# Queue orders in four places of a four-layer transformer kernel; the gate's exponential as a pow on GpSimd; gelu's table ahead of the norm; expert inputs halved off two banks

## The chip, the cores and the metric

One core of a Trainium2 chip runs the whole program as one launch. The metric is the device time in microseconds, as the median of several runs. TensorE (PE) multiplies matrices into PSUM banks of 128 x 512 f32; VectorE (DVE), ScalarE (ACT) and GpSimd (POOL) work element by element; SyncE (SP) issues the loads. Each engine works off its own queue in order and waits on semaphores.

## The reference, cut to what matters

The activations x are 2 x 256 tokens of 128 features, the context 2 x 512 x 128. Four layers follow one another, each a cross attention and a feed-forward part, all added to x:

```python
x = x + L0_xattn(layernorm(x), ctx, ctx, mask_ff1, ...)       # L0x: 16 heads of 64
x = x + L0_ffn(layernorm(x), tile_sigs, W, b)                 # L0f: one of 8 matrices per token
x = x + L1_xattn(layernorm(x), ctx, ctx, mask_bk0, ...)       # L1x: 16 heads of 8
x = x + L1_ffn(layernorm(x), ...)                             # L1f: self-attention, then 8 experts
x = x + L2_xattn(layernorm(x), ctx, ...)                      # L2x: 16 heads of 64
x = x + L2_ffn(layernorm(x), ...)                             # L2f: quantised product
x = x + L3_xattn(layernorm(x), ctx, ctx, ...)                 # L3x: one head of 128
x = x + L3_ffn(layernorm(x), ...)                             # L3f: small attention on 31 tokens
```

The parts that the change touches:

```python
# L0_ffn
scores = einsum('bsd,td->bst', x, sign(tile_sigs)); idx = argmax(scores, -1)
out = take_along_axis(einsum('bsd,tde->bste', x, W) + b, idx)
# L1_ffn
x = x + layernorm(attention(x, ...)) * ln1_g + ln1_b
probs = softmax(xt @ gate_w + gate_b)            # 8 experts
top_v, top_i = top_k(probs, 2); combine = sum(one_hot(top_i) * top_v)
for e in range(8):
    h = gelu(xt @ W1[e] + b1[e]) @ W2[e] + b2[e]
    out = out + combine[:, e:e + 1] * h
```

## The kernel before, in words

All work is laid out by hand: each engine has one program (`@block.tensor` and so on), and a stage is a function on each engine that runs in the order of the calls. There is no planner. `take` gives TensorE a PSUM bank once its last reader has freed it; `filled` and `emptied` are the two waits on a bank; `spare` issues products whose result nobody reads, in order to keep TensorE busy.

Tokens lie as 4 tiles of 128 rows (`X`, `XN`), or transposed as 128 x 512 (`XT`). The banks are S0 to S3, T0, T1, O and M. Products whose precision matters are made of f16 halves: a "high" is the value cast to f16 (ScalarE, `act_high`), a "low" is the rest (VectorE, `low`), and `PARTS` multiplies high by high, low by high and high by low, three passes into one bank. GpSimd's `split` makes both halves with two instructions: a product by one, and a subtraction.

The places that the change touches, in order of time:

- **Starts of L0x and L2x** (`pe_attention`, `project` L454, `pair_scores` L474, call at L575). TensorE makes the keys of the second pair of heads, K0(0,1), and then the scores of the first pair (j = 0 and 2). VectorE takes the maxima (L1668 in L2x) or looks for zeros (L1683 in L0x); in L2x it then halves the keys (L1703, L1708).
- **L0f and the way into L1x** (`pe_columns`, `pe_signatures`, `pe_l1x_kv`, `pe_l0f`, `pe_l1x`; VectorE's `l0f`, `l1x`). TensorE transposes bias columns, signs and four weights (bank T0), ScalarE copies the weights (L1459), TensorE projects the context to keys L1x.k0 and k1 (S0, S1). Then come the transposes of the normed rows (L867), the routing scores (L876), 8 routed products y0 to y7 (L889), VectorE's routed sum (L1901, 32 instructions). The keys are halved into `KN` by ScalarE (high) and VectorE (`l1x_low`); `pe_early_keys` repeats them for 4 heads at a time (RK, 8 pieces, L630), and ScalarE copies each out (L645). L1x's norm: VectorE's statistics, GpSimd's rstd (L2374, a pow by -0.5), VectorE's normed rows (L1605). Between statistics and normed rows VectorE has `small_loads` and the low of L2's value piece V0. TensorE then transposes (L385), fill value 2, query, fills 3 and 4, and the repeat of the query (RQ0, L654). GpSimd's queue: split of the routing weights, rstd of L0f, `selectors` (three memsets, six casts), rstd of L1x, then the splits of seven filled values, from a ring of four buffers `V32`.
- **Start of L1f** (`pe_l1f` L922): transposes, 6 spares, query, key and value projections, then `pe_packed`, which waits for the query, repeats it (RQ0), then repeats the key (RK0.0).
- **Into the experts** (`pe_l1f` L933 to L937, `act_moe` L1416, VectorE L1972 to L1984, GpSimd L2540 to L2547). The normed rows are transposed into bank M, ScalarE copies them to `XT[0]`, VectorE casts and subtracts (`halves`, L1629 and L1630) to get `X16`; TensorE computes the gate in f32 (L804), VectorE centres it (L1981) and finds the best expert (`best`, L1860 to L1864), ScalarE computes exp of the centred scores (L1418) and, per expert, gelu of four banks (L1426) and their highs (L1433); VectorE makes the lows (L1941) and splits W1 (L1947, L1949); GpSimd splits W2 (L2534, L2537) and adds the residual to X (L2545, L2547). VectorE finds the second expert, builds the factors (L1989 to L1996) and adds up (L2008, L2010).
- **Experts on TensorE** (`hidden` L946, `outputs` L958, `rounds`): hidden(i, k2 + 1), then outputs(i, k2). Five spares stand ahead of outputs(0, 0), four ahead of outputs(0, 1) and of the last outputs. `outputs` waits for all four hidden parts and goes token tile by token tile.

## Time and profile before

| | us |
|---|---|
| median of 3 runs | 552.6 (552.43 to 554.38) |
| the profiled execution | 552.83 |
| its span, first to last instruction | 551.1 |
| TensorE busy | 507.4 (92%) |
| VectorE busy | 432.0 (78%) |
| ScalarE busy | 341.0 (62%) |
| GpSimd busy | 271.3 (49%) |
| mean granted clock of TensorE | 0.994 |

Busy shares are means over stages with different limits. TensorE's figure includes the spare products. The stages in time: L0x until 148, L0f and the way into L1x until 180, L1x until 248, L1f's attention until 298, the experts until 355, L2x from 368 to 485, then L2f, L3x and L3f.

### The profile page before, as it was taken

What the parts mean: (1) busy time and instruction counts of PE and PEld (TensorE: products, weight loads), DVE (VectorE), ACT (ScalarE), POOL (GpSimd) and SP (SyncE); (2) the same over time, 40 slices, a digit from 0 to 9 for tenths busy, and PEclk for the clock granted to TensorE, in tenths of its full rate; (3) what the DMA queues carried; (4) which work ended last, traced back from release to release, by engine and by line L of the source; (5) the groups of instructions that cost most, each with busy time, mean ns of one, the idle gap of its engine ahead of it and who ended that gap; (6) DMA issues with size and microseconds to landing.
All of it is one profiled execution on the core that took longest, in us unless ns stands there. A gap on an engine that the chain in (4) does not pass through costs nothing.

```text
span 551.1 us, 13307 instructions
## 1 busy us (share of the span) xinstructions
PE 507.4 (92%) x4908; PEld 293.0 (53%) x4916; DVE 432.0 (78%) x1208; ACT 341.0 (62%) x682; POOL 271.3 (49%) x300
## 2 busy tenths in 40 slices
PE   8899999999897899999899799988999999999996
PEld 4345555567752233343334467735566656954574
DVE  7999999997584888827876899778777777587663
ACT  4688888888236366644662768538878888522212
POOL 7947777777622924410120443126888888500100
PEclk9989999999989999999999999999999999999999
DMA  9560000001120000000000222000000002000000
GB/s 236 133 175 8 1 2 3 1 2 41 51 103 1 1 1 2 2 1 0 2 1 21 77 77 58 2 1 1 2 1 3 1 2 78 3 0 1 2 0 20
DMA packets 24084, 15.43 MB, mean 28 GB/s; under 512 B 8083, under 2 KB 22230, under 8 KB 23894
## 3 DMA queue, kind: packets, MB, share of 16 engines
q1 hardware_dynamic: 24022, 14.60, 9.5%
q8 instruction: 39, 0.64, 0.5%
q14 instruction: 23, 0.19, 0.1%
HBM read 14.33 MB, written 0.26 MB: 26 GB/s over the span
## 4 chain that ended last, share of the span: by engine, by line
PE 51%; DVE 17%; issue 16%; POOL 9%; ACT 6%; DMA 1%; DVEq 0%; POOLq 0%; ACTq 0%
PE pspair L506 7%; PE psO L521 5%; PE psS L492 4%; PE psM L464 4%; PE pspair L967 4%; PE psO L720 3%; PE pspair L695 3%; DVE nmx L1788 2%; PE pspair L492 2%; ACT PP L1314 2%; POOL PP L2388 2%; PE pspair L954 2%; POOL PP L2385 2%; PE psS L669 1%; PE psS L954 1%
## 5 line engine op out<-in xcount | busy, mean ns | idle before, releaser
L506 PE MATMUL pspair<-ident,PP 128*128 128x128 f32 x512 | 82.1, 283 | 3.8 <-ACT PP L1314 3.7
L506 PEld LDWEIGHTS pspair<-ident,PP 128*128 128x128 f32 x512 | 54.2, 141 | 31.1 <-issue 21.7
L521 PE MATMUL psO<-V,PP 128*128 128x64 f16 x1536 | 65.7, 193 | 2.6 <-DVE Oall L1724 2.0
L521 PEld LDWEIGHTS psO<-V,PP 128*128 128x128 f16 x1536 | 59.8, 98 | 9.1 <-DVE PP L1690 2.9
L1690 DVE TENSOR_TENSOR PP<-pspair,PP 128x512 f16<-128x512 f32 x64 | 44.0, 688 | 25.7 <-ACT PP L1298 25.7
L1377 ACT ACTIVATE PP<-pspair 128x1024 f32<-128x1024 f32 x48 | 46.5, 1021 | 24.7 <-PE pspair L706 24.5
L2374 POOL TENSOR_TENSOR ln_rs<-ln_ve,minus_half 128x4 f32<-128x4 f32 x10 | 10.3, 1031 | 95.5 <-DVE ln_ve L1581 92.4
L1314 ACT ACTIVATE PP<-scores_m,nm 128x512 f32<-128x512 f32 x64 | 46.5, 727 | 5.5 <-DVE nm L1674 5.5
L2385 POOL TENSOR_TENSOR PP<-acc,one 128x512 f16<-128x512 f32 x32 | 33.3, 1040 | 31.7 <-ACT acc L1296 31.7
L2385 POOL TENSOR_TENSOR PP<-y_sb,one 128x512 f16<-128x512 f32 x32 | 33.3, 1040 | 16.9 <-ACT y_sb L1296 16.9
L2388 POOL TENSOR_TENSOR PP<-y_sb,PP 128x512 f16<-128x512 f32 x32 | 37.1, 1161 | 2.5
L2388 POOL TENSOR_TENSOR PP<-acc,PP 128x512 f16<-128x512 f32 x32 | 37.1, 1161 | 2.5
L1298 ACT CAST PP<-pspair 128x512 f16<-128x512 f32 x64 | 37.2, 581 | 0.6 <-PE pspair L506 0.6
L378 PE MATMUL pspair<-ident 128*128 128x512 f16 x136 | 34.3, 379 | 0.0
L464 PE MATMUL psM<-ctxTm,mask_i 128*128 128x512 f16 x99 | 27.5, 388 | 3.0 <-DVE Qst L1696 3.0
L1296 ACT COPY acc<-pspair 128x512 f32<-128x512 f32 x32 | 18.8, 587 | 13.2 <-PE pspair L506 13.2
L1296 ACT COPY y_sb<-pspair 128x512 f32<-128x512 f32 x32 | 18.8, 587 | 10.8 <-PE pspair L506 10.7
L720 PE MATMUL psO<-PP,Oall 128*9 128x256 f32 x384 | 25.2, 380 | 0.0
L1314 ACT ACTIVATE PP<-psS,nm 128x512 f32<-128x512 f32 x32 | 22.4, 699 | 3.5 <-DVE nm L1668 3.5
L1314 ACT ACTIVATE PP<-pspair,nm 128x512 f32<-128x512 f32 x32 | 22.3, 696 | 2.9 <-DVE nm L1668 2.9
L967 PEld LDWEIGHTS pspair<-scores_m,Oall 128*128 128x128 f16 x384 | 22.0, 98 | 2.2 <-issue 0.5
L1253 ACT COPY XT<-psM 128x512 f32<-128x512 f32 x7 | 4.1, 585 | 30.7 <-PE psM L385 30.7
(584 smaller groups left out, 1274.4 us busy)
## 6 DMA issues: line engine op xcount, KB each, us to landing
W<-in_L_ffn_W SPq DMA_DIRECT2D x16, 256.0 KB, 2.9
bigw<-in_L_xattn_w_q SPq DMA_DIRECT2D x2, 512.0 KB, 6.6
bigw<-in_L_xattn_w_kv SPq DMA_DIRECT2D x1, 1024.0 KB, 4.8
V<-in_ctx SPq DMA_DIRECT2D x1, 512.0 KB, 4.0
bigw<-in_L_xattn_w_v SPq DMA_DIRECT2D x1, 512.0 KB, 5.2
mask_b<-in_mask_BxS_ff SPq DMA_DIRECT2D x1, 512.0 KB, 7.1
bigw<-in_L_xattn_w_k SPq DMA_DIRECT2D x1, 512.0 KB, 6.1
bigw<-in_L_xattn_w_o SPq DMA_DIRECT2D x1, 512.0 KB, 3.9
```

The costliest lines, as they stand in the source:

```text
L464: mm = pe.matmul(bank["M"][:], (wq16 if what == "Q" else wk16)[:, wpart, cols_], X16[:, cpart, :] if what == "Q" else ctxTm16[:, cpart, keys],
L506: mm = pe.transpose(bank[f"T{j % 2}"][:, k * P:(k + 1) * P], Pb[j % 4][:, k * P:(k + 1) * P], ident[:])
L521: mm = pe.matmul(bank["O"][:, (j % UPH) * a.dv:(j % UPH + 1) * a.dv], (PTH, PTL)[ppart][j % 4][:, k * P:(k + 1) * P], (VH, VL)[vpart][:, b ...
L720: mm = pe.matmul(bank["O"][HR * j:HR * j + VR, b * S:(b + 1) * S], Vaug[:, b * kt + kc, HG * g + j, :], PX[(2 * r + j // 2) % 4][:, j % 2, ...
L967: mm = pe.matmul(bank[b][:, t * P:(t + 1) * P], HT16[k2][:, hpart, k, t * P:(t + 1) * P], W2h[k2][:, wpart, k * D:(k + 1) * D], start=(k = ...
L1296: nc.scalar.copy(P32[j // 2 % 2], ps[:]).then_inc(free[f"T{j % 2}"], 1)
L1298: nc.scalar.copy(PTH[j % 4][:, 0:a.keys], ps[:, 0:a.keys]).then_inc(sem(f"{n}.high"), 1)
L1314: nc.scalar.activation(Pb[j % 4][:, 0:a.keys], src[:, 0:a.keys], ACT.Exp, bias=nm[:, j % 4:j % 4 + 1], scale=-1.0 if a.mask else 1.0, accu ...
L1377: nc.scalar.activation(PX[k % 4], pairs[k % 2][:], ACT.Exp, scale=a.scale).then_inc(sem(f"{n}.exp"), 1)
L1690: dve.tensor_tensor(PTL[j % 4][:, 0:a.keys], ps[:, 0:a.keys], PTH[j % 4][:, 0:a.keys], ALU.subtract).then_inc(free[f"T{j % 2}"], 1)
L2385: pool.tensor_tensor(PTH[j % 4], P32[j // 2 % 2], one[:].broadcast_to([P, SK]), ALU.mult)\
L2388: pool.tensor_tensor(PTL[j % 4], P32[j // 2 % 2], PTH[j % 4], ALU.subtract)\
```

## The change

It reorders queues, moves work between engines and takes out spares. In the diff below "..." marks what is left out; left out are the removal of `l1x_low`, the allocation of `zero16`, `gate16` and `euler` and their two memsets on GpSimd, and the new bank names.

```diff
 def pe_attention
-            project("K0", 0, 1)
             for j in (0, 2):
                 pair_scores(0, j)
+            project("K0", 0, 1)
 def pe_early_keys
-                emptied(pe, f"L1x.k{c}")
+                pe.wait_ge(sem("L0.vsplit"), 5 + c)
 def pe_packed   (repeat of the key first, then of the query; ScalarE's copies likewise)
+            if halves:
+                emptied(pe, f"{n}.k")
+                repeat_k(pe, 0, 0, take(pe, f"{n}.RK0.0", "S3"), full["S3"])
+            emptied(pe, f"{n}.q")
+            ps = take(pe, f"{n}.RQ0", "S2")
+            repeat_q(0, ps, full["S2"])
 def pe_l1x_keys   (was pe_columns, pe_signatures, pe_l1x_kv)
             ...                                    # the four transposes of weights
             mm.then_inc(full["T0"], 1)
+            pe_columns(pe)
+            pe_signatures(pe)                       # bank T1, was S3
             emptied(pe, "L1x.wT")
             for g in range(2):
                 pe_one(pe, f"L1x.k{g}", f"S{g}", sqT[:, 1, :], ctxT[:, g * 512:(g + 1) * 512])
 def pe_l0f
-                    pe_early_keys(pe, range(0, 2))
+                    pe_early_keys(pe, range(0, 1))
...
             pe_onehot_rows(pe, "L0f", route_b)
+            pe_early_keys(pe, range(1, 3))
             pe_l1x_mask(pe)                         # bank S0, was T0
-            pe_early_keys(pe, range(2, 8))
+            pe_early_keys(pe, range(3, 8))
 def pe_l1x
-            pe_wide_values(pe, "L2", range(0, 2), "T0 T1")
+            pe_wide_values(pe, "L2", range(0, 1), "S1 S2")
...
             pe_ln(pe, "L1x", XN[0])
-            pe_fill_value(pe, 2, "S3")
+            pe_wide_values(pe, "L2", range(1, 2), "S1 S2")
             emptied(pe, "L1x.xt")
             pe_one(pe, "L1x.q", "M", sqT[:, 0, :], XT[0][:])
-            pe_fill_value(pe, 3, "S1")
+            pe_fill_value(pe, 2, "S3")
+            pe_fill_value(pe, 3, "S0")
             pe_fill_value(pe, 4, "T0")
 def pe_l1f
-            spare(pe, "T1", 6)
+            spare(pe, "T1", 4)
...                                                 # key, then query (was query, key)
             spare(pe, "S0", 16)
-            pe_ln(pe, "L1g", XN[0])
-            spare(pe, "S0", 3)
-            emptied(pe, "L1g.xt")
-            pe.wait_ge(sem("ld.moe"), 2 * 16)
-            pe_tiles(pe, "L1f.gate", "M", lambda t: XT[0][:, t * P:(t + 1) * P], lambda t: gate_w[:], E)
+            for h, b in enumerate(("M", "S3")):
+                ps = take(pe, f"L1g.xt{h}", b)
+                for t in range(2):
+                    pe.wait_ge(sem("L1g.xn"), 2 * h + t + 1)
+                    mm = pe.transpose(ps[:, t * P:(t + 1) * P], XN[0][:, 2 * h + t, :], ident[:])
+                mm.then_inc(full[b], 1)
+            spare(pe, "S0", 2)
+            for h in range(2):
+                emptied(pe, f"L1g.xt{h}")
+            pe.wait_ge(sem("gate"), 1)
+            ps = take(pe, "L1f.gate", "M")
+            for t in range(NT):
+                for m, (xpart, wpart) in enumerate(PARTS):
+                    mm = pe.matmul(ps[:, t * E:(t + 1) * E], X16[:, xpart, t * P:(t + 1) * P], gate16[:, wpart, :],
+                                   start=(m == 0), stop=(m == 2))
+            mm.then_inc(full["M"], 1)
+            def last_outputs(i):
+                b, base = at["moe.y1"]
+                pe.wait_ge(free[b], base + i)
+                pe.matmul(bank[b], zero16[:], ident16[:].unsqueeze(1).broadcast_to([P, 4, P]), start=True, stop=False)
+                pe.wait_ge(sem("moe.w2"), 2 * i + 2)
+                for k in range(NF):
+                    emptied(pe, f"moe.h{k}", 2 * i + 1)
+                    for t in range(NT):
+                        for m, (hpart, wpart) in enumerate(PARTS):
+                            mm = pe.matmul(bank[b][:, t * P:(t + 1) * P], HT16[1][:, hpart, k, t * P:(t + 1) * P],
+                                           W2h[1][:, wpart, k * D:(k + 1) * D],
+                                           start=False, stop=(k == NF - 1 and t == NT - 1 and m == 2))
+                mm.then_inc(full[b], 1)
...                                                 # used for the last expert; the spares of 5, 4 and 4 are gone
 ScalarE
-            act_high(act, f"L1x.k{g}", KN[:, g * 512:(g + 1) * 512])
+            act_copy(act, f"L1x.k{g}", V32[g])
-            nc.scalar.activation(pr8[:], sc8[:], ACT.Exp).then_inc(sem("moe.exp"), 1)
...                                                 # mask copy at n == 3, V0 and V1 behind L1x.xt, then the query
             act_out(act, L1F, 1)
-            act_copy(act, "L1g.xt", XT[0][:])
+            nc.scalar.activation(warm[:], one[:], ACT.Gelu)
+            for h in range(2):
+                act_high(act, f"L1g.xt{h}", X16[:, 0, h * 256:(h + 1) * 256], n=256)
 VectorE
-                ln("L1x", X, XN[0], [small_loads] + lows("L2", range(0, 1)))
-                wide_low("L2", 1)
+                ln("L1x", X, XN[0], [small_loads])
+                for step in lows("L2", range(0, 2)):
+                    step()
...
-                packed(L1X, [l3_angles])
+                packed(L1X, [l3_angles, gate_halves])   # gate_halves: gate_w to gate16, two instructions
...
-                emptied(dve, "L1g.xt")
-                halves(X16[:, 0, :], X16[:, 1, :], XT[0][:]).then_inc(sem("moe.x"), 1)
+                for h in range(2):
+                    low(f"L1g.xt{h}", X16[:, 1, h * 256:(h + 1) * 256], X16[:, 0, h * 256:(h + 1) * 256], n=256)
 GpSimd
+            selectors()
             rstd("L0f")
-            selectors()
+            pool.wait_ge(sem("L0f.factors"), 1)
+            for g, c in enumerate(halves):
+                emptied(pool, f"L1x.k{g}")
+                split(KN[:, c], KN[:, CTX + g * 512:CTX + (g + 1) * 512], V32[g], "L0.vsplit", g + 5)
             rstd("L1x")
...
-            pool.wait_ge(sem("moe.x"), 1)
+            for h in range(2):
+                emptied(pool, f"L1g.xt{h}")
             for k2 in range(2):
                 split_W2(0, k2, True)
+            pool.wait_ge(sem("moe.centred"), 1)
+            pool.tensor_tensor(pr8[:], euler[:].unsqueeze(2).broadcast_to([P, NT, E]), sc8[:], ALU.pow)\
+                .then_inc(sem("moe.exp"), 1)
```

## Rows read from the trace of the kernel before

**Rows 1.** The page, part 4: shares of the chain that ended last, by engine.

```profile
PE 51%; DVE 17%; issue 16%; POOL 9%; ACT 6%; DMA 1%; DVEq 0%; POOLq 0%; ACTq 0%
```

**Rows 2.** Timeline of VectorE, start of the first attention: start, us, engine, line, instruction, [idle before <-releaser].

```profile
25.20 1.29 DVE L1683 TENSOR_SCALAR Zt<-psS 128x512 bf16<-128x512 f32 x2 [0.22 <-PE psS L492]
```

**Rows 3.** Windows: length, busy us of PE, PEld, DVE, ACT, POOL, granted clock, DMA share, GB/s.

```profile
28.50:31.90 3.40, 3.40 (x14) 0.96 (x11) 2.27 (x8) 2.48 (x6) 0.00 (x0) 0.51 0.27 64
...
148.00:151.40 3.40, 1.92 (x11) 1.21 (x11) 3.17 (x18) 0.58 (x1) 0.55 (x1) 1.00 0.58 178
151.40:154.80 3.40, 3.40 (x10) 1.75 (x9) 1.02 (x4) 0.98 (x2) 3.33 (x10) 0.50 1.01 376
...
323.60:351.20 27.60, 27.60 (x309) 20.11 (x308) 26.12 (x52) 22.00 (x40) 10.85 (x10) 1.00 0.17 49
```

**Rows 4.** Timeline of TensorE from the end of the first attention on.

```profile
148.24 0.25 PE L827 MATMUL psO<-ident,vec 39*128 39x39 f32 x1
...
150.75 3.16 PE L809 MATMUL psS<-ctxT,sqT 128*128 128x512 f32 x4 [0.68 <-ACT sqT L1253]
...
173.85 1.01 PE L385 MATMUL psM<-ident,XN 128*128 128x128 f32 x4 [0.82 <-DVE XN L1605]
...
178.27 0.59 PE L654 MATMUL pspair<-qT,Oall 128*128 128x512 f16 x2
```

**Rows 5.** Timeline of VectorE, the same stages.

```profile
150.68 0.87 DVE L1872 TENSOR_SCALAR XN<-X,ln_mv 128x128 f32<-128x128 f32 x4
...
157.73 2.16 DVE L1901 SCALAR_TENSOR_TENSOR X<-psS,pr,X 128x128 f32<-128x128 f32 x8
...
172.75 0.69 DVE L1624 TENSOR_TENSOR V<-pspair,V 128x512 f16<-128x512 f32 x1 [3.96 <-ACT V L1260]
```

**Rows 6.** Timeline of GpSimd, the same stages.

```profile
151.82 0.96 POOL L2432 MEMSET Oall<- 128x1024 f32 x1
...
168.61 1.05 POOL L2374 TENSOR_TENSOR ln_rs<-ln_ve,minus_half 128x4 f32<-128x4 f32 x1 [13.81 <-DVE ln_ve L1581]
```

**Rows 7.** Timeline of ScalarE, the same stages.

```profile
170.09 1.26 ACT L645 ACTIVATE scores_m<-pspair,key_one 128x512 f16<-128x512 f32 x2 [0.20 <-PE pspair L630]
```

**Rows 8.** Timeline of TensorE, start of the self-attention (L1f).

```profile
253.46 1.02 PE L809 MATMUL psM<-XT,sq 128*128 128x512 f32 x2
...
258.57 0.40 PE L669 MATMUL psS<-Oall,Qst 24*128 24x256 f16 x4
```

**Rows 9.** Timeline of ScalarE, start of the mixture of experts.

```profile
306.00 1.28 ACT L1426 ACT_TABLE_LOAD   x1
```

**Rows 10.** Timeline of VectorE, the same stage.

```profile
303.86 0.69 DVE L1630 TENSOR_TENSOR XT<-XT 128x512 f16<-128x512 f32 x1
...
305.98 0.98 DVE L1861 TENSOR_TENSOR eq<-sc,rank 128x32 f32<-128x32 f32 x1
...
309.22 0.69 DVE L1941 TENSOR_TENSOR Oall<-psS,Oall 128x512 f16<-128x512 f32 x1
...
321.85 1.13 DVE L2008 TENSOR_SCALAR acc<-pspair,oh 128x128 f32<-128x128 f32 x4
```

**Rows 11.** Timeline of GpSimd, the same stage.

```profile
305.75 1.16 POOL L2537 TENSOR_TENSOR scores_m<-W,scores_m 128x512 f16<-128x512 f32 x1
```

**Rows 12.** Timeline of TensorE, the experts.

```profile
313.28 1.24 PE L378 MATMUL psM<-ident 128*128 128x512 f16 x5
...
351.26 1.03 PE L378 MATMUL psM<-ident 128*128 128x512 f16 x4
```

**Rows 13.** Groups of GpSimd instructions by form: count, busy us, mean ns.

```profile
L2374 POOL TENSOR_TENSOR ln_rs<-ln_ve,minus_half 128x4 f32<-128x4 f32 x10 | 10.3, 1031 | 95.5 <-DVE ln_ve L1581 92.4 <-DVE ln_ve L1578 3.2
...
L2566 POOL TENSOR_TENSOR ss<-ss,s_half 64x1 f32<-64x1 f32 x1 | 0.5, 541 | 21.6 <-DVE ss L2313 21.6
```

**Rows 14.** Timeline of TensorE, start of the last attention (L2x).

```profile
368.54 1.13 PE L468 MATMUL psM<-ctxT,bigw 128*128 128x512 f32 x2 [0.20 <-DVE Qst L1621]
```

**Rows 15.** Timeline of VectorE, the same stage.

```profile
370.46 1.29 DVE L1668 TENSOR_REDUCE nm<-psS 128x1 f32<-128x512 f32 x2 [1.97 <-PE psS L492]
```

More of the change, by code:

```diff
@@ L244, in build @@
         gate_w = sb("gate_w", [P, E])
+        gate16 = sb("gate16", [P, 2, E], F16)
+        euler = sb("euler", [P, 1])
         b2w = sb("b2w", [E, D])
@@ L732, in pe_packed @@
             halves = 0 if a.mask else B * a.keys // 512
-            emptied(pe, f"{n}.q")
             pe.wait_ge(sem("sel"), 5)
-            ps = take(pe, f"{n}.RQ0", "S2")
-            repeat_q(0, ps, full["S2"])
             if halves:
@@ L830, in pe_signatures, with pe_l1x_keys @@
             pe.wait_ge(sem("L0f.sign"), 1)
-            ps = take(pe, "L0f.sigT", "S3")
-            pe.transpose(ps[:, 0:E], signs[:, 1, :], ident[0:E, 0:E]).then_inc(full["S3"], 1)
-        def pe_l1x_kv(pe):
+            ps = take(pe, "L0f.sigT", "T1")
+            pe.transpose(ps[:, 0:E], signs[:, 1, :], ident[0:E, 0:E]).then_inc(full["T1"], 1)
+        def pe_l1x_keys(pe):
             pe.wait_ge(sem("ld.L1x"), 4 * 16)
@@ L853, in pe_l1x_mask @@
         def pe_l1x_mask(pe):
-            ps = take(pe, "L1x.mask", "T0")
+            ps = take(pe, "L1x.mask", "S0")
             pe.wait_ge(sem("mask"), 1)
@@ L859, in pe_l1x_mask @@
                                       mask_n[:, q, k * P:(k + 1) * P], identb[:])
-            mm.then_inc(full["T0"], 1)
+            mm.then_inc(full["S0"], 1)
         def pe_l0f(pe):
@@ L973, in rounds @@
                 for k2 in range(2):
-                    if not (last and k2 == 1):
-                        hidden(i, k2 + 1)
-                    else:
-                        spare(pe, "M", 4)
+                    if last and k2 == 1:
+                        last_outputs(i)
+                        continue
+                    hidden(i, k2 + 1)
                     outputs(i, k2)
-            pe.wait_ge(sem("moe.x"), 1)
             hidden(0, 0)
             hidden(0, 1)
-            spare(pe, "M", 5)
             outputs(0, 0)
             hidden(0, 2)
-            spare(pe, "M", 4)
             outputs(0, 1)
@@ L1377, in exps @@
                 nc.scalar.activation(PX[k % 4], pairs[k % 2][:], ACT.Exp, scale=a.scale).then_inc(sem(f"{n}.exp"), 1)
+            for c in range(halves):
+                repeated_k(0, c)
             repeated_q(0)
@@ L1381, in act_packed @@
                 act_fill_value(act, 5)
-            for c in range(halves):
-                repeated_k(0, c)
             for r in range(-a.lead, a.rounds + 2):
@@ L1473, in _ @@
                 act_repeated_k(act, Kaug, "L1x", n // 2, n % 2)
-            act_wide_values(act, "L2", range(0, 2))
             act.wait_ge(sem("ld.short"), 16 * len(SHORT))
@@ L1482, in _ @@
             act_copy(act, "L1x.xt", XT[0][:])
+            act_wide_values(act, "L2", range(0, 2))
+            act_high(act, "L1x.q", q16[:, 0:TOK], scale=float(DN) ** -0.5)
             act_fill_value(act, 2)
-            act_high(act, "L1x.q", q16[:, 0:TOK], scale=float(DN) ** -0.5)
             act_fill_value(act, 3)
@@ L1864, in best @@
                 return dve.tensor_tensor(dst[:], eq8[:], rank[:].unsqueeze(2).broadcast_to([P, NT, E]), ALU.is_equal)
-            def l1x_low(g):
-                low(f"L1x.k{g}", KN[:, CTX + g * 512:CTX + (g + 1) * 512], KN[:, g * 512:(g + 1) * 512])
             def l0f():
@@ L1956, in l1f @@
                 emptied(dve, "vec")
+                low("L1f.k", KN[:, CTX:CTX + TOK], KN[:, 0:TOK], bias=colp["L1_ffn_bk"])
                 low("L1f.q", q16[:, TOK:2 * TOK], q16[:, 0:TOK], bias=colp["L1_ffn_bq"])
-                low("L1f.k", KN[:, CTX:CTX + TOK], KN[:, 0:TOK], bias=colp["L1_ffn_bk"])
                 ps = filled(dve, "L1f.v")
```

21 lines of the change are left out of this document (11 added, 10 removed).

## Prediction

> **What bounds it now.** I read the page's chain of waits first. TensorE holds 51% of it, VectorE 17% and "issue" 16% [rows 1]; loads hold almost nothing. So the middle of each attention is TensorE's and the change hardly touches it; what it can win lies at the stage borders, where every engine waits on a chain of small steps. I then read the timeline of each engine around the six places that the diff touches, and the windows for the clock. The profiled execution took 552.83 us (span 551.1, 1.73 around it); the median of the three runs, 552.6, is 0.2 below it, so I sum against 552.83 and take 0.2 off. "Same" below means within 0.5% (2.8 us), about what a measurement of this kernel tells from no change.
>
> **1. Scores ahead of the key projection (L0x).** Before the first scores TensorE runs K0(0,1). VectorE starts on the scores at 25.20 after 0.22 idle [rows 2]; until then it drained values. The swap can give back only that 0.22; VectorE's queue is the next limit. The key's copy on ScalarE stands behind the first exp and isn't late. Term: -0.2. Bounds: 0 to -1.6, because at 28.50 to 31.90 the granted clock is 0.51 (the 1.2 GHz level) after a stretch in which TensorE mostly waited [rows 3]. The moved projection fills part of that wait. Were the clock to stay up, the half of the 3.4 us stretch that is lost would shrink until VectorE (busy 2.27 of 3.40 there) binds, about 1.35. I leave it out of the sum.
>
> **2. L0f and the start of L1x.** Four edits with one answer.
> Before: columns at 148.24, then the signatures' transpose waits for bank S3, the weights' transposes (0.66), ScalarE's copy, the two key projections at 150.75 for 3.16, so to 153.91 [rows 4]. The normed rows were begun at 150.68 and done at 151.55 [rows 5], so their transposes stood 2.2 us behind the keys. The keys are long since the clock was 0.50 in 151.40 to 154.80, after 1.92 busy of 3.40 [rows 3]; at full clock a pair of such passes takes about 0.86 (an estimate: two 512-column f32 passes take 1.02 with their overlapping end [rows 8]), so 1.7 for both.
> After: weights' transposes at 148.24 (no S3 to wait for), the two small ones beside ScalarE's copy, keys about 149.75. TensorE's wait shrinks from about 1.4 to 0.6, so I take it that the clock holds: keys done 151.5, normed transposes 151.95, scores, argmax, and the routed sum begins near 154.9 instead of 157.73 [rows 5]: -2.8. VectorE's two key rests leave its queue; they lay in waits.
> What pays: selectors() (0.96 memset first, 2.9 in all, from 151.82 [rows 6]) now runs from about 146.5, beside VectorE's mask preparation and the X additions. The rows show that VectorE's instructions with SBUF operands wait for a GpSimd instruction (item 5). Bounds 0 to +0.9 (memset alone); I take +0.4.
> The key halves go to GpSimd, behind L0f.factors: four instructions, 1.04 and 1.16 each by the same split elsewhere (the second is 1.16 [rows 11]; two instructions 1.12 apart), 4.5 us from 154.7 to 159.2. Cover: VectorE's routed sum reads PSUM, and L0f's rstd is ahead of them, L1x's far behind. First user is RK0.0 at about 158.7, which needs the first half (157.0): no wait. rstd for L1x follows in the queue and would start near 165.7.
> Then the larger half: rstd was ready at 168.61 + 1.05 = 169.66 [rows 6], but the normed rows stood in VectorE's queue behind the rest of V0, which ran only at 172.75 after 3.96 idle [rows 5]; TensorE transposed at 173.85 [rows 4]. Moved behind, that 3.7 goes. What is late next is ScalarE's key copies: the last pair ran 170.09 to 171.35 [rows 7], at 0.65 each; by the new order (mask third, banks S0) they end near 168.3, then three tiny activations, and the transposed copy at 168.95 (174.9 before). V1 stands ahead of the query on TensorE (0.86), fills 2 to 4 behind it (2.6). RQ0 comes at about 173.2 against 178.27 [rows 4]: -5.1, with the +0.4: **-4.7**. GpSimd starts splitting the fills 4 us sooner, so it stays ahead of its ring of four. Bounds: -2.8 (clock still low, selectors fully in the way) to -5.6.
>
> **3. L1f.** Spares 6 to 4 (0.43), key before query, its repeat first. From 253.46 (query) to the first narrow products at 258.57 [rows 8] is a chain of two projections, high, rest, repeat, copy. It starts 0.4 sooner; the last member is now the query, of the same form. **-0.4**, bounds 0 to -0.5.
>
> **4. Gelu's table.** Loaded at 306.00 for 1.28 [rows 9] between exp and the first gelu; now it runs in ScalarE's idle time behind the output copy, and exp is gone from ScalarE. First gelu near 304.8 instead of 307.30.
>
> **5. Halves of two banks, gate, pow.** X16 was ready at 303.86 + 0.69 = 304.55 [rows 10]; cast, copy and rest on two half tiles, the first under the second transposes, end about 303.6. Gate is 12 f16 products (about 0.45). Then VectorE binds: argmax instructions wait for GpSimd. The one at 305.98 took 0.98 [rows 10] and ended 0.05 after GpSimd's of 305.75 + 1.16 = 306.91 [rows 11]; uncontended such ones take 0.19. GpSimd's splits start 1.0 earlier and so end earlier; the first low, 309.22 [rows 10], comes at 308.4: only -0.8 of the 2.5 that gelu gained. The second hidden layer follows, and with the five spares at 313.28 (1.08 before the next product [rows 12]) gone, outputs(0,0) is 2.8 earlier. But the loop is VectorE's too (from 323.60 to 351.20 TensorE is busy for all 27.60, VectorE for 26.12 [rows 3]), and it enters it with the first sum, 321.85 [rows 10], which needs the factors. What sets those is GpSimd's new queue: split W2 twice (to 308.3), **pow**, X additions 2.6, W2 of the next expert 2.3.
> Pow on 32 elements isn't in the trace. 128x4 took 1.031, 64x1 0.541 [rows 13]: 0.163 per further element, so 0.54 + 31 x 0.163 = 5.6; below, 1.0 (all overhead), above 32 x 0.541 = 17.3. At 5.6 it ends at 313.9. The exponentials aren't needed before 319, but the two additions and the W2 split then fall on VectorE's W1(1,1) split and second argmax, which they hold up some 3 us where 1.6 were lost before. The first sum comes at 321.4: **-0.5**. At 1.0 the additions lie earlier: -2.0. If pow also holds VectorE's SBUF operands off for all its 5.6, W1(1,0) waits: +1.7.
> A rule of the Trainium skill bears here (SBUF — State Buffer, "SBUF: two separate sides" and "Who interferes with whom"): a GpSimd instruction that reads SBUF and a VectorE one with two SBUF inputs or in a two-port mode exclude each other for the whole instruction. The trace agrees for the argmax (0.98, not 0.19); by the rule alone pow would hold the port all along, which is rival A.
>
> **6. Last expert by k.** Zero product, then each hidden part as it comes. The four spares at 351.26 and the wait to 352.37 (1.1 [rows 12]) go, the zero product costs 0.2: **-0.9**, bounds -0.7 to -0.9. VectorE was waiting for that bank.
>
> **7. L2x.** Scores are 1.1 earlier (the projection of 368.54, 1.13 [rows 14]), the maxima too; but the key's copy, third on VectorE, now waits for the projection behind two pairs of scores, near 371.05 instead of 370.46 + 1.2 = 371.66 [rows 15]. **-0.6**, bounds 0 to -1.1.
>
> Two extra memsets at the start lie in a GpSimd wait. No load moves except with the stages.
>
> Sum: 0.2 + 4.7 + 0.4 + 0.5 + 0.9 + 0.6 = 7.3; 552.83 - 7.3 = 545.5, as a median 545.3. Ends of all terms: 11.7 and 1.8 saved (540.9 and 550.8).
>
> **Rivals.**
> A. Pow holds VectorE's SBUF port for its 5.6 us. For: the argmax rows. Against: the 128x4 pows run beside VectorE products of SBUF operands (L1587) that keep their length. Item 5 is +1.7 instead of -0.5: 547.5.
> B. L0f's gain is eaten: selectors delay X by 0.9, the clock stays at its low level, so item 2 is -2.8: 547.2. For: the clock fell there once. Against: less waiting ahead of it.
> C. Slower: pow costs its upper price, 17.3, and holds the port. W1(1,0), due at 310.9, ends at 326.7, where hidden(0,2) stood at 317.04 (313.28, 1.08 of spares, 2.68 of outputs): +9.7, and the lows, split and argmax queued behind it meet the additions (+2): +11.7 for item 5, less 6.8: 557.5. It beats the gain from a pow of about 12.5 us. Against: two points of pow lie far below.
> D. Both clock dips vanish and pow is short: 552.6 - 10.5 = 542.1.
> E. The gelu load isn't kept (copies between warm-up and gelu bring another table): item 4 back. VectorE binds there anyway, so about 0.5: 545.8, inside the forecast.
>
> **Chances.** Forecast (with E) 0.60, A 0.14, B 0.12, D 0.10, C 0.04. Its own range is 543.5 to 547; with A, B and most of D 541.8 to 549. Faster 0.89 (all but C and the worst joint cases of A and B), same 0.08, slower 0.03.
>
> **What would show it.** The routed sum 2.4 us earlier after the attention; clock 1.00 there; V0's rest behind the normed rows; no idle before XN beyond rstd; the pow's own row (near 5.6), VectorE's casts beside it either 0.42 or stretched; the table load before 300; no spares between the experts and 0.9 less before the last sum. Wrong would be: gaps before RK0.0 for the key halves, or a first sum later than before relative to the stage's start.

## The result, and the profile after

The changed kernel takes 546.88 us in the median of 7 runs (545.62 to 549.77). The kernel before, run beside it, takes 551.73 (551.40 to 554.38). The ratio is 0.991, with a 95% interval of 0.9884 to 0.9935: 4.9 us faster. I had forecast 545.3, in a range of 541.8 to 549. The profiled execution took 547.37 (span 545.7), 5.5 less than that of before, where the sum said 7.3. The ratios here and below leave out the few executions that took over 1.5% longer than the fastest of their kernel; the medians include them. All the differences below are between these two traces, each counted from its first instruction.

How far ahead of the kernel before the changed one is, at seven places:

| place | before | after | ahead |
|---|---|---|---|
| zeros of the third pair of heads, L0x | 32.12 | 31.00 | 1.12 |
| bias added to X, end of L0x | 147.55 | 147.55 | 0.00 |
| routed sum, L0f | 157.73 | 154.88 | 2.85 |
| repeated query RQ0, L1x | 178.27 | 172.93 | 5.34 |
| narrow products, L1f | 258.57 | 254.74 | 3.83 |
| first and last sum of the experts | 321.85, 355.25 | 317.88, 350.31 | 3.97, 4.94 |
| key copy of L2x | 371.66 | 366.22 | 5.44 |

VectorE after the last unit of L0x (start, us, engine, line, instruction, [idle before <-releaser]):

```profile
145.61 1.13 DVE L1680 TENSOR_SCALAR mask_n<-acc 128x512 bf16<-128x512 f32 x1
146.67 0.84 DVE L1680 TENSOR_SCALAR mask_n<-y_sb 128x512 bf16<-128x512 f32 x1
147.55 0.69 DVE L2382 TENSOR_TENSOR X<-X,rows 128x512 f32<-128x512 f32 x1
...
154.88 2.16 DVE L1923 SCALAR_TENSOR_TENSOR X<-psS,pr,X 128x128 f32<-128x128 f32 x8
...
166.85 1.12 DVE L1632 TENSOR_SCALAR XN<-X,ln_mv,ln_rs 128x128 f32<-128x128 f32 x4 [0.91 <-POOL ln_rs L2401]
...
364.50 1.29 DVE L1695 TENSOR_REDUCE nm<-psS 128x1 f32<-128x512 f32 x2 [0.94 <-PE psS L495]
366.22 0.69 DVE L1730 CAST Amat<-psM 128x512 f16<-128x512 f32 x1 [0.43 <-PE psM L471]
```

GpSimd beside it, and in the experts:

```profile
145.41 1.06 POOL L2459 MEMSET Oall<- 128x1024 f32 x1
...
154.70 1.05 POOL L2504 TENSOR_TENSOR kT<-ctxTm,one 128x512 f16<-128x512 f32 x1 [2.82 <-DVE oh L1891]
...
304.47 5.42 POOL L2578 TENSOR_TENSOR pr<-euler,sc 128x32 f32<-128x32 f32 x1
309.86 1.26 POOL L2582 TENSOR_TENSOR X<-X,XN 128x512 f32<-128x512 f32 x1
```

The third zeros and the mask instructions of the kernel before, for comparison:

```profile
32.12 1.29 DVE L1683 TENSOR_SCALAR Zt<-psS 128x512 bf16<-128x512 f32 x2 [1.35 <-PE psS L492]
...
146.75 0.43 DVE L1653 TENSOR_SCALAR mask_n<-acc 128x512 bf16<-128x512 f32 x1
147.09 0.42 DVE L1653 TENSOR_SCALAR mask_n<-y_sb 128x512 bf16<-128x512 f32 x1
```

The first memset now lies on VectorE's two mask instructions, which took 0.43 and 0.42 in the kernel before. They take 1.13 and 0.84, and the 1.12 that L0x had won is gone at 147.55. In L0f and L1x the picture is the forecast one. The normed rows stand behind rstd alone (0.91 idle, where 3.96 stood ahead of V0's rest [rows 5]), and the key halves on GpSimd keep nobody waiting.

TensorE, and the windows (length; busy us of PE, PEld, DVE, ACT, POOL; granted clock; DMA share; GB/s):

```profile
148.71 1.95 PE L812 MATMUL psS<-ctxT,sqT 128*128 128x512 f32 x4 [0.76 <-DVE X L2385]
...
172.93 0.59 PE L657 MATMUL pspair<-qT,Oall 128*128 128x512 f16 x2
...
249.74 1.10 PE L812 MATMUL psS<-XT,sq 128*128 128x512 f32 x2 [0.69 <-DVE V L1651]
250.67 1.02 PE L812 MATMUL psM<-XT,sq 128*128 128x512 f32 x2
...
305.43 2.54 PE L972 MATMUL psS<-XT,scores_m 128*128 128x512 f16 x6 [2.40 <-DVE Oall L1968]
```

```profile
25.20:28.50 3.30, 2.00 (x10) 0.56 (x9) 3.30 (x10) 1.04 (x3) 3.22 (x3) 1.00 0.59 135
28.50:31.90 3.40, 3.38 (x23) 1.98 (x24) 3.40 (x11) 3.19 (x9) 0.07 (x1) 1.00 0.28 68
...
179.40:182.80 3.40, 1.95 (x6) 0.53 (x6) 3.30 (x8) 0.58 (x1) 3.24 (x4) 1.00 0.00 0
182.80:186.20 3.40, 3.20 (x9) 0.82 (x10) 2.26 (x9) 0.58 (x1) 3.32 (x4) 0.50 0.00 0
302.20:305.60 3.40, 1.00 (x5) 0.32 (x4) 3.26 (x6) 3.37 (x7) 3.32 (x4) 1.00 0.46 155
305.60:309.00 3.40, 3.40 (x9) 1.20 (x8) 2.50 (x5) 1.66 (x3) 3.40 (x1) 0.51 0.26 77
```

Both stretches at the 1.2 GHz level [rows 3] are gone: the key projections take 1.95 instead of 3.16 [rows 4]. Two new ones stand at the first maxima of L1x and at the second hidden layer. The first costs 1.2: the maxima behind it are 5.34 ahead on its near side and 4.13 on its far side. At L1f TensorE waits 0.69 for VectorE to free bank S0, ahead of the key; the query, which came first before, needed only bank M.

The head of the experts, on VectorE:

```profile
301.35 0.98 DVE L1888 TENSOR_TENSOR eq<-sc,rank 128x32 f32<-128x32 f32 x1
...
304.59 1.29 DVE L1968 TENSOR_TENSOR Oall<-psS,Oall 128x512 f16<-128x512 f32 x2
...
307.00 0.42 DVE L1974 CAST scores_m<-W 128x512 f16<-128x512 f32 x1
307.45 0.69 DVE L1976 TENSOR_TENSOR scores_m<-W,scores_m 128x512 f16<-128x512 f32 x1
...
312.74 1.21 DVE L1974 CAST scores_m<-W 128x512 f16<-128x512 f32 x1
...
313.99 1.53 DVE L1976 TENSOR_TENSOR scores_m<-W,scores_m 128x512 f16<-128x512 f32 x1
...
317.88 1.13 DVE L2035 TENSOR_SCALAR acc<-pspair,oh 128x128 f32<-128x128 f32 x4
...
350.31 0.35 DVE L2037 SCALAR_TENSOR_TENSOR acc<-pspair,oh,acc 128x128 f32<-128x128 f32 x1 [1.10 <-PE pspair L986]
```

Beside the pow (304.47 to 309.89) the W1 split has its plain lengths, 0.42 and 0.69. Beside the W2 split (312.63 to 314.97), which follows the two X additions, the next one takes 1.21 and 1.53.

### The profile page after: what moved, and what is told of

It reads as the page before. It is cut to its first block and busy times, and to the rows that moved or that the text cites. A ratio compares the mean times of both kernels' runs of the same rounds, so it can differ in the third digit from the quotient of the medians.

```text
span 545.7 us, 13308 instructions
## 1 busy us (share of the span) xinstructions
PE 503.3 (92%) x4905; PEld 289.4 (53%) x4905; DVE 431.3 (79%) x1208; ACT 341.1 (63%) x683; POOL 282.0 (52%) x307
## 5 line engine op out<-in xcount | busy, mean ns | idle before, releaser
L1695 DVE TENSOR_REDUCE nm<-psS 128x1 f32<-128x512 f32 x32 | 21.4, 673 | 0.9 <-PE psS L495 0.9
L1695 DVE TENSOR_REDUCE nm<-pspair 128x1 f32<-128x512 f32 x32 | 21.8, 681 | 0.0
```

Of the source, the lines that this page charges most:

```text
L1695: dve.tensor_reduce(nmc, ps[:, 0:a.keys], AX.X, ALU.max, negate=True)\
```

## The experiments

Each was timed in five rounds beside the kernel before. That kernel's median was 553.6 to 553.8 in these sets, and 551.7 beside the changed kernel. In these sets 37 of its 52 executions had a mean granted clock of 0.991 or less; those at 0.994, the clock of its profiled execution, took 551.4 to 552.7, but for one of 554.6. So by the clock most of its executions have at least one stretch at the lower level more than its trace shows. Ratios are against the before of the same set, and the changed kernel was in none of them. One set is not like another: exp_back below has the changed kernel's median, 546.88, but stood 6.7 under the kernel before in its set, where the changed kernel stood 4.9 under. What an edit does to the changed kernel is therefore read from the traces.

**l0f_alone.** The kernel before with place 2 alone:

```diff
+            selectors()
             rstd("L0f")
-            selectors()
+            pool.wait_ge(sem("L0f.factors"), 1)
+            for g, c in enumerate(halves):
+                emptied(pool, f"L1x.k{g}")
+                split(KN[:, c], KN[:, CTX + g * 512:CTX + (g + 1) * 512], V32[g], "L0.vsplit", g + 5)
...
-                ln("L1x", X, XN[0], [small_loads] + lows("L2", range(0, 1)))
+                ln("L1x", X, XN[0], [small_loads])
...
```

> The kernel before with place 2 of the change alone (L0f and the start of L1x: the memset block early, key halves on GpSimd, weights' transposes ahead of the small ones, V0's rest behind the normed rows). Theory from the two traces: the routed sum begins at about 154.9 to 155.3 (157.73 before), the first repeated query near 173.3 (178.27), and a stretch at half clock of about 3.4 us stands at the first maxima of L1x and takes back some 1.2, so the whole execution saves 3.5 to 4.2. Rival 1 (the recorded term holds whole, no half clock at L1x): saves 4.7 or more. Rival 2 (the half clock comes from the other places and the collision with the mask preparation shows in full, since nothing ahead was won): saves 2.5 to 3.3, with X plus its output rows 0.8 to 1.1 later than before.

549.64, ratio 0.9935 (0.9913 to 0.9957), 3.6 less by the ratio; its profiled execution 4.15 less than that of before. Its windows, with the same columns as above:

```profile
25.20:28.50 3.30, 1.05 (x11) 0.48 (x10) 3.26 (x10) 1.31 (x4) 2.72 (x3) 1.00 0.58 131
28.50:31.90 3.40, 3.40 (x25) 1.81 (x23) 3.40 (x10) 3.19 (x8) 0.12 (x1) 1.00 0.31 74
```

RQ0 comes at 172.66, and the half clock stands at 184.2 to 187.6; at the maxima behind it 4.16 of the 5.6 are left. So the theory was right about the half clock there. The size is another matter: 1.39 of the 5.6 was won in L0x, where the clock stayed in this trace (third zeros at 30.73 against 32.12), and not by the edit. Place 2 by itself is worth 4.2 at RQ0 and 2.8 behind the maxima. That is the range of rival 2, and its reason is seen too: the mask instructions take 1.14 and 0.85 beside the memset. The windows hold a surprise: ahead of 28.5 TensorE was as idle as in the kernel before (1.05 busy against 1.04), and here the clock stayed.

**sel_late.** The changed kernel with the memset block back behind rstd:

```diff
-            selectors()
             rstd("L0f")
+            selectors()
```

> The changed kernel with the block of memsets and copies (L2459 on) moved back behind rstd of L0f. Theory: in the changed kernel VectorE's mask preparation beside the first memset takes 1.13 + 0.84 instead of 0.43 + 0.42, and that ate 1.1 that had been won ahead of it; without it L2382 and everything behind comes 1.0 to 1.1 earlier, so 0.8 to 1.1 less than the changed kernel. Rival (the block is then in the way of the key halves, or stretches VectorE's argmax in L0f): X is 1.1 earlier but the routed sum is not, or the first repeated query waits for the keys: 0 to +0.5 against the changed kernel.

545.68, ratio 0.9876 (0.9836 to 0.9916). VectorE:

```profile
145.05 0.43 DVE L1680 TENSOR_SCALAR mask_n<-acc 128x512 bf16<-128x512 f32 x1
145.40 0.42 DVE L1680 TENSOR_SCALAR mask_n<-y_sb 128x512 bf16<-128x512 f32 x1
145.85 0.69 DVE L2382 TENSOR_TENSOR X<-X,rows 128x512 f32<-128x512 f32 x1
```

X is 1.70 ahead of the changed kernel where 0.55 came in from earlier: 1.15 for this edit, and it stays to the end. (The intervals of this run and of the changed kernel overlap; the reading rests on the traces.) The move of the block was pure loss; nothing behind it needed it early.

**l1f_bank.** The changed kernel with two banks exchanged:

```diff
-            pe_one(pe, "L1f.k", "S0", sq[:, 5, :], XT[1][:])
-            pe_one(pe, "L1f.q", "M", sq[:, 4, :], XT[1][:])
+            pe_one(pe, "L1f.k", "M", sq[:, 5, :], XT[1][:])
+            pe_one(pe, "L1f.q", "S0", sq[:, 4, :], XT[1][:])
```

> The changed kernel with L1f's key on bank M and its query on bank S0. Theory: the key projection waited 0.69 for bank S0, which VectorE frees only with the rest of the twelfth wide value; on M it starts at once, and the first narrow products of L1f come 0.6 to 0.7 earlier relative to the stage's transposes. Rival (VectorE's queue of rests is what binds, so the key's rest comes no earlier): first narrow products move by 0.2 or less.

548.11, ratio 0.9889 (0.9856 to 0.9923). TensorE at L1f:

```profile
248.58 1.01 PE L388 MATMUL psM<-ident,XN 128*128 128x128 f32 x4 [0.46 <-DVE XN L1632]
...
250.35 1.10 PE L812 MATMUL psM<-XT,sq 128*128 128x512 f32 x2
...
255.35 0.39 PE L672 MATMUL psS<-Oall,Qst 24*128 24x256 f16 x4
```

From the transposes to the narrow products it is 6.77, where the changed kernel has 254.74 - 247.17 = 7.57: 0.8 for the bank. The kernel before has 7.25. The median doesn't show it; the clock hides at least a part: in this profiled execution TensorE had half clock for 10.2 us from 182.0 on, and its six executions spread from 544.28 at a mean clock of 0.997 to 550.62 at 0.986 (another at 0.997 took 547.25, so the clock isn't all of the spread).

**spares.** The changed kernel with idle products in the two waiting places:

```diff
+                if a.mask and r == -1:
+                    ring_spare(pe, a, 5)
                 if (r + 1) % rpi == 0 and 0 <= (r + 1) // rpi < NG * B:
                     turn_max((r + 1) // rpi)
...
             hidden(0, 0)
+            spare(pe, "M", 9)
             hidden(0, 1)
```

> The changed kernel with idle products in the two places ahead of its half-clock stretches: 5 of 0.22 before the first transposed maxima of L1x (idle there 1.35), 9 of 0.22 between the first two hidden layers (idle there 2.4). Theory: both stretches keep clock 1.00; L1x's gives back about 1.2 of time, the experts' 0.0 to 0.5, since VectorE binds there: 1.2 to 1.7 less than the changed kernel. Rival 1: the clock falls in the next stretch instead, and nothing is won (within 0.3). Rival 2: the products themselves are on the path and cost 0.3 to 1.

548.72, ratio 0.9906 (0.9889 to 0.9923). Both stretches kept clock 1.00 and the rests of the second hidden layer came 2.85 ahead of the changed kernel's. Then all was lost, in TensorE's idle time ahead of the loop:

```profile
313.60:317.00 3.40, 0.76 (x14) 0.58 (x11) 3.09 (x10) 0.72 (x2) 2.21 (x2) 1.00 0.47 154
317.00:320.40 3.40, 2.59 (x8) 0.95 (x9) 3.37 (x9) 0.00 (x0) 0.00 (x0) 0.50 0.26 77
```

VectorE's factors were not ready (second argmax and factors from 312.34 to 317.00, held up by GpSimd's W2 splits), so TensorE waited, and the clock fell for the first two turns of a loop that TensorE binds. The last sum is 1.6 behind the changed kernel's. This is rival 1, and worse than it said. It names the real limit of this stage: the factors.

**exp_back.** The changed kernel with exp on ScalarE again, no pow and no early table:

```diff
-            nc.scalar.activation(warm[:], one[:], ACT.Gelu)
+            act.wait_ge(sem("moe.centred"), 1)
+            nc.scalar.activation(pr8[:], sc8[:], ACT.Exp).then_inc(sem("moe.exp"), 1)
...                                                 # GpSimd's pow is gone
```

> The changed kernel with the gate's exponential as Exp on ScalarE again and without the early load of gelu's table, so ScalarE loads exp's and gelu's table ahead of the first gelu (before: 1.28 for one load at 306.00), and GpSimd goes from the first two W2 splits straight to the X additions. Theory (VectorE binds the head of the experts): the first gelu comes some 2 to 3 later, the first rests on VectorE about 1 to 2 later, and the first sum 0 to 1 later relative to the stage's start; whole kernel within 1 of the changed one. Rival A, pow holds VectorE's port: then without it the first rests and the W1(1,0) split are shorter (they are 1.29 and 0.42 + 0.69 with pow beside them) and the first sum comes 1.5 or more earlier.

546.88, ratio 0.9869 (0.9841 to 0.9897). ScalarE and, after it, VectorE's first rests:

```profile
301.06 0.23 ACT L1446 ACTIVATE pr<-sc 128x32 f32<-128x32 f32 x1 [1.78 <-DVE sc L2010]
301.31 1.28 ACT L1454 ACT_TABLE_LOAD   x1
302.61 1.24 ACT L1454 ACTIVATE psS<-psS,cols 128x512 f32<-128x512 f32 x2
```

I had written two table loads; there is one, exp's is the table in place. The first gelu is 1.5 later (302.61 against 301.12), but the first rest starts at 304.53 against 304.59, since VectorE is held by its argmax until then, and the first sum comes at 317.67 against 317.88. So gelu's table and the pow together bring nothing in the changed kernel. Rival A falls too.

**pow2.** The changed kernel with the pow twice, VectorE waiting for the second:

```diff
-                dve.wait_ge(sem("moe.exp"), 1)
+                dve.wait_ge(sem("moe.exp"), 2)
...
+            pool.wait_ge(sem("moe.exp"), 1)
+            pool.tensor_tensor(pr8[:], euler[:].unsqueeze(2).broadcast_to([P, NT, E]), sc8[:], ALU.pow)\
+                .then_inc(sem("moe.exp"), 1)
```

> The changed kernel with the power computed twice, one behind the other, with VectorE waiting for the second. The duration of one was 5.42, so GpSimd's queue (the X additions, the W2 split of the next expert) moves 5.5 later. Theory: pow doesn't hold the port and has slack; the W1(1,1) split (now 1.21 + 1.53 beside the additions) runs at 0.42 + 0.69 beside the second power, but the factors wait for that power, due at about 315.4, and then meet the additions, so the first sum moves by -0.5 to +1.5 and the whole kernel by as much. Rival (pow is dear wherever it stands, holds the port, or delays the W2 splits that outputs(1,0) needs): +3 to +5.5.

547.77, ratio 0.9908 (0.9875 to 0.9941). GpSimd:

```profile
303.90 5.42 POOL L2578 TENSOR_TENSOR pr<-euler,sc 128x32 f32<-128x32 f32 x1
309.40 5.42 POOL L2581 TENSOR_TENSOR pr<-euler,sc 128x32 f32<-128x32 f32 x1
314.77 1.27 POOL L2585 TENSOR_TENSOR X<-X,XN 128x512 f32<-128x512 f32 x1
```

The first sum is at 317.48, 13.46 behind the first rest, where the changed kernel has 13.29. A whole further pow costs 0.2 there: the queue has that slack, and what the W1 split gains (1.11 instead of 2.74) the factors lose again on the additions.

**head.** The changed kernel with the second argmax beside the pow, and the additions behind GpSimd's loop:

```diff
+                link(dve.scalar_tensor_tensor(out=rk8[:], in0=oh8[:], scalar=-BIG, in1=sc8[:], op0=ALU.mult, op1=ALU.add))
+                link(best(rk8, rk8))
+                link(dve.tensor_tensor(oh8[:], oh8[:], rk8[:], ALU.add))
                 hidden_low(0, 1)
                 split_W1(1, 1)
-                link(dve.scalar_tensor_tensor(out=rk8[:], in0=oh8[:], scalar=-BIG, in1=sc8[:], op0=ALU.mult, op1=ALU.add))
-                link(best(rk8, rk8))
-                link(dve.tensor_tensor(oh8[:], oh8[:], rk8[:], ALU.add))
...                                                 # GpSimd's loop of W2 splits ahead of the two X additions
```

> The changed kernel with VectorE's second argmax (7 small instructions, 1.5 in all) ahead of the rests of the second hidden layer, beside the power, where VectorE had 2.0 of idle time, and with GpSimd's two X additions behind its loop instead of ahead of it. Theory: the W1(1,1) split is no longer held up (1.1 instead of 2.74), the factors are ready by about 315 instead of 317.9, and the first sum is bounded by TensorE's outputs(0,1), which end at 317.8: -0.1 to -0.5 for the first sum, up to -1.2 if TensorE gets ahead through the earlier rests of hidden(0,2); whole kernel 0.3 to 1.2 less. Rival (GpSimd's W2 splits now fall on what the additions fell on, and the additions meet the end of the experts): within 0.3, or slower by up to 1.

544.69, ratio 0.9831 (0.9801 to 0.9861). The median is 2.2 less than the changed kernel's, but the interval overlaps that of exp_back in the same set, so the trace has to carry the reading. VectorE:

```profile
307.93 0.18 DVE L2014 SCALAR_TENSOR_TENSOR rk<-oh,sc 128x32 f32<-128x32 f32 x1
...
312.04 0.42 DVE L1974 CAST scores_m<-W 128x512 f16<-128x512 f32 x1
...
314.39 1.13 DVE L2035 TENSOR_SCALAR acc<-pspair,oh 128x128 f32<-128x128 f32 x4
```

The first sum is 3.49 earlier, much more than expected: it needs outputs(0,0), done at 312.4, and not outputs(0,1), which I had named. TensorE's own order then binds (outputs(0,1) end at 317.7), and the last sum is 1.7 earlier (348.60). The run moves two things, the argmax and the additions; what each gives by itself wasn't run.

**combo.** sel_late, l1f_bank, spares and head together.

> The changed kernel with all four: the memset block behind rstd of L0f (-1.7 of which -1.15 its own in its profile), L1f's key on bank M (-0.65), idle products in the two waiting places, and the reordered head of the experts. Theory: each is kept, and with the factors early TensorE doesn't wait 2.8 ahead of the loop as it did with the idle products alone, so the half clock doesn't fall into the loop: 541.5 to 543.5, that is 3.5 to 5.5 under the changed kernel. Rival: the half clock comes in another stretch, and with it 1.2 to 3 of that is lost: 544 to 546.5.

540.71 (five of six executions at 540.50 to 541.60), ratio 0.9797 (0.9749 to 0.9844): faster than both kernels (the changed kernel's fastest was 545.62), and below what I expected. The trace shows clock 1.00 from 7.6 to the end; here is the head of the experts:

```profile
299.00:302.40 3.40, 2.93 (x15) 1.20 (x13) 3.30 (x6) 2.79 (x6) 3.32 (x3) 1.00 0.52 170
302.40:305.80 3.40, 3.40 (x38) 2.34 (x36) 3.16 (x11) 3.30 (x6) 3.40 (x1) 1.00 0.30 79
```

**combo_bare.** The same without the 14 idle products.

> The best version so far (540.7; clock at 1.00 throughout) without its idle products in the two waiting places. Theory (the idle products keep the clock): one or two stretches at half clock, at the first maxima of L1x and at the second hidden layer, 1.2 to 3 more: 541.9 to 543.7. Rival (the clock fell there for other reasons and the idle products do nothing): within 0.3 of 540.7.

542.34, ratio 0.9815 (0.9788 to 0.9842), 1.6 more than combo. Its profiled execution, which took 545.63, has half clock at 182.8 to 193.0 and at 305.7 to 309.1:

```profile
182.80:186.20 3.40, 2.64 (x15) 0.72 (x14) 1.28 (x5) 0.93 (x2) 3.12 (x3) 0.50 0.00 0
```

In the traces the clock goes with the idle products: the second hidden layer fell to half clock in 6 of the 7 traces with the new experts and without them (in l1f_bank the fall came later, at 322.0), and in none of the 3 with them. That the 1.6 is the clock's isn't shown. The intervals of the two overlap, and one execution of combo_bare had a mean clock of 1.000 and still took 542.34, while three at 0.997 took 542.0 to 542.1. So the clock can hold without the idle products, and where the 1.6 comes from stays open.

**combo_exp.** combo with exp back on ScalarE.

> The best version so far with the gate's exponential back on ScalarE and both tables loaded at the head of the experts. In the changed kernel this made no difference that its runs told (546.9 both). Theory: VectorE's factors no longer bind the head, so ScalarE's later gelu now shows: the first rests 0.5 to 1.5 later and the first sum too, +0.5 to +1.5 (541.2 to 542.2). Rival (GpSimd's queue, freed of 5.4, gives that back): -0.3 to +0.3.

541.40, ratio 0.9808 (0.9782 to 0.9833), with the clock at 1.00 too. The first sum is at 311.89 against combo's 311.02, and 0.84 of that 0.87 is left in the profiled executions (541.34 against 540.50), 0.7 in the medians. The ratios don't tell the two apart, so this rests on the traces, both at clock 1.00: pow and the early table are worth 0.7 to 0.8 once VectorE's factors are out of the way, as the theory said, and nothing while they bind.

**last_alone** and **swap_alone.** The kernel before with the last outputs by k alone, and with the order of scores and key projection alone:

```diff
-                    if not (last and k2 == 1):
-                        hidden(i, k2 + 1)
-                    else:
-                        spare(pe, "M", 4)
+                    if last and k2 == 1:
+                        last_outputs(i)
+                        continue
+                    hidden(i, k2 + 1)
```

```diff
-            project("K0", 0, 1)
             for j in (0, 2):
                 pair_scores(0, j)
+            project("K0", 0, 1)
```

> The kernel before with the last expert's output by k alone (zero product, then each hidden part as it comes; the 4 idle products gone). Theory: from the first sum of the experts to the last 32.5 instead of 33.4, so -0.9 for everything behind. Rival (VectorE's sums bind, or the clock falls since the idle products are gone): 0 to -0.4.

> The kernel before with the first two pairs of scores ahead of the key projection in L0x and L2x alone. Theory: 0 to -0.3 in L0x beside what the clock does, -0.5 in L2x (its key's rest is what comes next), together -0.5 to -0.8. Where the stretch 28.5 to 31.9 is at half clock or not isn't the swap's doing, since the kernel with L0f's part alone kept it at 1.00 after the same 1.05 busy of 3.30. Rival (the swap fills the wait and keeps the clock): L0x by itself 1.1 to 1.4 earlier in nearly all executions, and the median some 1.7 to 2 lower.

552.86, ratio 0.9977 (0.9952 to 1.0002), and 552.96, ratio 0.9992 (0.9971 to 1.0013): too small for the timer. In the traces, the last two sums of the experts in the kernel before and in last_alone:

```profile
352.14 1.12 DVE L2010 SCALAR_TENSOR_TENSOR acc<-pspair,oh,acc 128x128 f32<-128x128 f32 x4
355.25 1.13 DVE L2010 SCALAR_TENSOR_TENSOR acc<-pspair,oh,acc 128x128 f32<-128x128 f32 x4 [1.99 <-PE pspair L967]
...
354.65 1.11 DVE L2026 SCALAR_TENSOR_TENSOR acc<-pspair,oh,acc 128x128 f32<-128x128 f32 x4
356.87 1.13 DVE L2026 SCALAR_TENSOR_TENSOR acc<-pspair,oh,acc 128x128 f32<-128x128 f32 x4 [1.10 <-PE pspair L969]
```

They are 3.11 apart in the kernel before and 2.22 in last_alone, so -0.89, and 2.22 in the changed kernel too (348.09 to 350.31). From the first sum to the last, the measure that I had named, last_alone takes 32.86 against 33.40, only -0.54: a W1 cast between the first sum and the second took 1.04 instead of 0.69.

At L2x swap_alone goes from its last sum (356.26) to the key copy (372.15) in 15.89, where before has 355.25 to 371.66, so 16.41: -0.5. In L0x it has clock 1.00 at 28.5 and is 1.37 ahead there, as the rival said; the rival's drop of the median is not seen. Its profiled execution took 559.37 with a mean clock of 0.978, but the long stretch at half clock lies from 529.1 to 542.8, behind both places.

## Why the prediction came out as it did

The sign, the range and most terms were right; the saving was overestimated, 7.3 against 4.9 by the medians. The traces give 5.4 up to the key copy of L2x; against the sum, by terms: 0.9 more in L0x, 0.5 less in L0f with L1x's start, 1.2 lost to the clock in L1x, 0.7 less in L1f, 0.4 less at the head of the experts.

1. **L0x (-0.2 forecast, -1.1 measured).** The bound of -1.6 was the better number, and so was the price of 1.35 beside it: counted from the first zeros (25.20 before, 25.52 now, since VectorE's value rests began later) the third are 1.44 earlier. The swap's own 0.2 isn't seen; all of the gain goes with the clock. The moved projection doubled TensorE's busy time there (2.00 of 3.30, was 1.04) and the half clock at 28.5 went. It is absent in all 11 traces with the new order, present in 2 of the 3 with the old one; l0f_alone is the exception, so the order makes the fall unlikelier rather than being its only condition.
2. **L0f and the start of L1x (-4.7 forecast, -4.2 measured).** Both mechanisms held: the routed sum at 154.88 (154.9 forecast), RQ0 at 172.93 (173.2). The half clock behind the attention, at the key projections, stands in all 3 traces with the old L0f and in none of the 11 with the new. But selectors cost 1.15, not 0.4: I had bounded it by one memset, 0.9, and two VectorE instructions waited. By luck item 1's unforecast gain of the same size hid the error. Then came what no step had: half clock at the first maxima of L1x, +1.2. TensorE's idle time there (1.95 busy of 3.40) was about as long in the kernel before (2.00 of 3.40 from 184.5), where the clock held in the profiled execution and fell in those of last_alone and swap_alone. Without idle products all 8 traces with the new L1x fall there, with them none of 3; but single executions without them reached a mean clock of 1.000 (pow2 546.13, head 542.42, combo_bare 542.34), so the fall isn't certain. Most executions of the kernel before also have a stretch more than its trace, and 2 of the 3 traces with the old L1x fall at these maxima. So the 1.2 is a loss against this one trace of the kernel before, and only in part the doing of the change. I had looked for clock only where it was already low.
3. **L1f (-0.4 forecast, +0.3 measured).** The failed step. I called the two projections alike and didn't ask when each one's bank comes free; the row in the result has TensorE waiting 0.69 for the key's bank, S0. From the transposes to the narrow products the stage takes 7.25 before, 7.57 in the changed kernel and 6.77 in l1f_bank, so with the bank exchanged the forecast gain is there.
4. **Gelu's table.** As forecast, hidden; it was loaded at 292.7 and kept, which settles E. The first gelu is 6.2 ahead, 2.3 more than L1f was, and that is worth nothing by itself (exp_back).
5. **Head of the experts (-0.5 forecast, -0.1 measured).** Pow took 5.42 against my 5.6, and VectorE did bind, by the argmax and the held-up W1(1,1) split. The first rest was 0.8 ahead of what L1f had left, as forecast. Half clock in the second hidden layer (its two groups of products take 2.54 and 2.11, and 1.67 and 1.47 in the kernel before) then delayed VectorE's next rests: at the W1(1,1) split only 0.1 of the 0.8 is left (316.71 and 312.74). From there to the first sum both kernels take 5.14. I had expected GpSimd to hold VectorE up by 3 there, where 1.6 were lost before; it was 1.6 again, only on the split (2.74 instead of 1.11) and no longer on the argmax. Keeping the clock wouldn't have saved the term: in spares, where it held, GpSimd's splits met the factors, and the first sum came 14.22 behind the first rest instead of 13.29. The fall at the second hidden layer isn't new with the change either: last_alone and swap_alone have it, with the old experts.
6. **Last expert (-0.9 forecast, -0.89 twice).** Right. (From the first sum to the last it is -0.97 in the changed kernel and -0.54 in last_alone; the W1 casts in between differ.)
7. **L2x (-0.6 forecast, -0.5 twice).** Right.

The rivals: A fell with the split at 0.42 and 0.69 beside the pow. The Trainium skill (SBUF — State Buffer, "Who interferes with whom") has a two-port VectorE mode and any GpSimd instruction shut each other out for the whole instruction: by that rule the trace agrees for the memset (1.13 instead of 0.43), but not for pow, where VectorE's cast of W keeps its 0.42, though the same cast takes 1.21 beside the W2 split. B was half right, with the price of selectors and not with the clock. C is excluded by the 5.42. D was right about both old stretches, and wrong in that two others came and that pow wasn't short; its two conditions are worth 1.35 and 1.5 above the 7.3, so 10.2 and not the 10.5 that I wrote.

The median is no clean measure of a term here. Executions of the changed kernel took 545.62 at a mean clock of 0.997 and 548.58 at 0.988, more than most single edits move; one at 0.994 took 549.77, which the mean clock doesn't explain and which stays open.

## What to carry to other kernels

When an edit removes idle time, look at every place where the matrix engine still waits, and not only at those where its clock was low: it may fall at the next one. A few idle products in the wait went with a kept clock in all three traces that had them, but in spares the time was lost again, because what followed waited for another engine, and what they saved elsewhere isn't settled. One trace is one execution: before a stretch at half clock is booked as the cost of a change, see how often the old kernel has it. When a block of work is moved on GpSimd, list the VectorE instructions that it will now lie beside, all of them, and when two equal projections change places, check which bank each needs and who frees it. Before moving an operation off an engine, find what binds the stage: here the pow and the early table were worth nothing, then 0.7 to 0.8 once the small factor chain had moved into the idle time beside the pow.

## What the runs showed of the hardware that I had not expected

- GpSimd's pow on 128x32 takes 5.42, against 1.03 for 128x4, and VectorE's split of SBUF operands beside it keeps its plain lengths (0.42, 0.69), whereas beside a GpSimd product or subtraction it takes 1.2 and 1.5.
- A GpSimd memset, which reads nothing, holds up a VectorE tensor_scalar from SBUF to SBUF: 1.13 instead of 0.43.
- The same code with the same idle time (1.04 and 1.05 busy of 3.30) was followed by half clock in one kernel and full clock in another. Most stretches at half clock lasted 3.4 us, but there is one of 6.8 (spares), two of 10.2 (l1f_bank, combo_bare) and one of 13.7 (swap_alone).
